# First feed-forward: three bf16 parts of its inputs in place of float32, and rows turned back one step further on

## The reference

```python
def act_quant(x):
    scale = 127.0 / jnp.clip(jnp.max(jnp.abs(x), axis=-1, keepdims=True), 1e-05)
    return jnp.clip(jnp.round(x * scale), -128, 127) / scale
def weight_quant(w):
    scale = 1.0 / jnp.clip(jnp.mean(jnp.abs(w)), 1e-05)
    return jnp.clip(jnp.round(w * scale), -1, 1) / scale
h = bit_linear(x, w1)                       # 256 -> 1024, both sides quantised
h = silu(depthwise_conv1d(h, conv_w, conv_b))   # 3 taps along the 1024 positions
return bit_linear(h, w2)                    # 1024 -> 256
```

## Time and profile before

| | us |
|---|---|
| median of 3 runs | 1917.15 (1917.0 to 1918.5) |
| profiled execution | 1919.29 |
| its span, first to last instruction | 1917.6 |
| the stage, L456 first to last update | about 185.9 to 454 |
| PE busy in the span | 1650.0 (86%) |
| DVE, ACT, POOL busy | 1160.5 (61%), 882.6 (46%), 321.8 (17%) |

### The profile page before, as it was taken

How to read it: one execution, slowest core, us unless ns; L and a number is a source line. 1 busy time by engine, 2 the same in 40 slices (tenths; PEclk the granted TensorE clock), 3 DMA queues, 4 the chain that set the end, 5 groups by cost and what they waited for, 6 DMA issues and landing times. The chain is left out here.

```text
span 1917.6 us, 29587 instructions
## 1 busy us (share of the span) xinstructions
PE 1650.0 (86%) x10149; PEld 1250.2 (65%) x10149; DVE 1160.5 (61%) x2579; ACT 882.6 (46%) x1795; POOL 321.8 (17%) x359
## 2 busy tenths in 40 slices
PE   7797789887899898799997489999936999979998
PEld 5454345556676665688885289999935888854446
DVE  4668567676456566889886823222257898842116
ACT  2332577764532221466653355555544666533213
POOL 0000000000000001211100345555562111001110
PEclk9898899998899999999998689999977999979999
DMA  6000000003000000100004812222261000010002
GB/s 200 1 1 1 1 1 1 1 1 126 1 1 1 1 1 1 31 2 1 2 1 162 322 59 72 73 73 70 72 198 28 1 2 1 2 47 0 0 1 89
DMA packets 62849, 78.83 MB, mean 41 GB/s; under 512 B 13179, under 2 KB 52655, under 8 KB 62319
## 3 DMA queue, kind: packets, MB, share of 16 engines
q1 hardware_dynamic: 42967, 47.35, 7.4%
q0 software_dynamic: 7584, 20.72, 3.4%
q10 hardware_dynamic: 12152, 8.85, 1.5%
HBM read 58.16 MB, written 18.74 MB: 40 GB/s over the span
## 5 line engine op out<-in xcount | busy, mean ns | idle before, releaser
L3003 PEld LDWEIGHTS moe_bank<-moe_xt,moe_w1e 128*128 128x128 f32 x1264 | 155.0, 194 | 5.8 <-DVE moe_xt L2851 1.8
L3003 PE MATMUL moe_bank<-moe_xt,moe_w1e 128*128 128x128 f32 x1264 | 155.8, 277 | 1.1 <-DVE moe_xt L2851 1.1
L3013 PE MATMUL moe_bank<-moe_w,moe_xin 128*128 x632 | 149.3, 379 | 0.0
L3077 ACT ACTIVATE moe_xin<-moe_bank,moe_b 128x128 f32<-128x128 f32 x316 | 90.3, 368 | 125.0 <-PE moe_bank L3003 124.9
L372 PE MATMUL l0f_hb<-l0f_xt,f_w 128*128 128x512 f32 x256 | 125.8, 623 | 5.3 <-DVE l0f_a L306 3.8
L1472 POOL TENSOR_TENSOR all_x<-all_x,l1x_fbias 128x256 f32<-128x256 f32 x32 | 23.4, 735 | 597.6 <-DVE l1x_fxn L204 597.6
L3013 PEld LDWEIGHTS moe_bank<-moe_w,moe_xin 128*128 128x128 f32 x632 | 114.0, 190 | 12.3
L209 DVE BATCH_NORM_STATS2 all_stats<-all_x 128x6 f32<-128x256 f32 x256 | 104.0, 421 | 5.2
L2860 DVE TENSOR_TENSOR moe_y<-moe_bank,moe_b2r 128x256 f32<-128x256 f32 x79 | 33.5, 425 | 118.7 <-PE moe_bank L3013 118.7
L2920 POOL DMA_INDIRECT moe_results<-moe_y,moe_row x79 | 78.0, 988 | 125.1 <-DVE moe_y L2860 121.8
L2851 DVE COPY moe_xt<-moe_bank 128x256 f32<-128x256 f32 x79 | 33.6, 425 | 106.6 <-PE moe_bank L2991 106.6
(11 more groups left out here) (484 smaller groups left out, 3812.7 us busy)
## 6 DMA issues: line engine op xcount, KB each, us to landing
moe_w<-in_L_ffn_W SPq DMA_DIRECT2D x32, 512.0 KB, 10.5
moe_w<-moe_results SPq DMA_DIRECT2D x16, 512.0 KB, 8.7
all_x<-in_x SPq DMA_DIRECT2D x4, 1024.0 KB, 12.6
out_x<-all_x SPq DMA_DIRECT2D x8, 512.0 KB, 2.9
f_w<-in_L_ffn_w_T SPq DMA_DIRECT2D x2, 1024.0 KB, 13.1
moe_inputs<-moe_xin ACTq DMA_DIRECT2D x8, 256.0 KB, 7.2
moe_inputs<-moe_w1e ACTq DMA_DIRECT2D x8, 256.0 KB, 7.8
moe_b2r<-in_L_ffn_b SPq DMA_DIRECT2D x1, 2048.0 KB, 14.1
```

What stands on the lines that cost most here:

```text
L3003: ins = nc.tensor.matmul(out, w1e[:, at:at + P], xt[:, u, c * P:(c + 1) * P], start=(c == 0), stop=(c == DC - 1))
L3013: ins = nc.tensor.matmul(bank[4 + u][:, 0:D], ht[:, u, c * P:(c + 1) * P], w2[:, ds(e * (HC * D) + c * D, D)], start=(c == 0), stop=(c == ...
L3077: ins = nc.scalar.activation(ht[:, u, m * P:(m + 1) * P], bank[1 + u][:, m * P:(m + 1) * P], ACT.Gelu, bias=b1[:, ds(e * HC + m, 1)])
```

## The change

The turned inputs are kept as float32 `xt` for one batch and as three bf16 planes `xs`: the value rounded to bf16, the rest rounded to bf16, and the rest of that. Each half of `up` is now DC x 3 = 6 bf16 matmuls against w1 in bf16 (`w1b`). For the first batch ScalarE and VectorE make the planes; for the others GpSimd does, with four instructions in a chain for each pair of tiles; `up` waits for `xs_ready`. `turn_back`, `copy_q` and `down` work on tile t-2 in place of t-1, `update` and `stats` on t-3, and there is one step more. `zq` has two buffers. ScalarE does copy_q of half 0 ahead of quantise_x and centre.

```diff
-                for t in range(TB):
+                def rest(t):
+                    dve.wait_ge(s.xt_ready, t + 2)
+                    nc.vector.tensor_tensor(rows(t), rows(t), plane(t, 0), ALU.subtract).then_inc(s.rest_ready, 2)
+                def low(t):
+                    dve.wait_ge(s.mid_ready, t + 2)
+                    nc.vector.tensor_tensor(plane(t, 2), rows(t), plane(t, 1), ALU.subtract).then_inc(s.xs_ready, 2)
...
+                for t in range(0, TB + 2, 2):
+                    if t < TB:
+                        rest(t)
+                    if t >= 2:
+                        low(t - 2)
                 norm_range(nc, c, sh, TB, T)
...
+            @block.gpsimd
+            def _(pool):
+                k = Chain(pool, s.split_step)
+                for t in range(TB, T, 2):
+                    pool.wait_ge(s.xt_ready, t + 2)
+                    if t % TB == 0 and t >= 2 * TB:
+                        pool.wait_ge(s.h_ps, (t // TB - 1) * M)
+                    k.link(nc.gpsimd.tensor_copy(plane(t, 0), rows(t)))
+                    k.link(nc.gpsimd.tensor_tensor(rows(t), rows(t), plane(t, 0), ALU.subtract))
+                    k.link(nc.gpsimd.tensor_copy(plane(t, 1), rows(t)))
+                    nc.gpsimd.tensor_tensor(plane(t, 2), rows(t), plane(t, 1), ALU.subtract).then_inc(s.xs_ready, 2)
...
                     if half == 0:
-                        pe.wait_ge(s.xt_ready, (b + 1) * TB)
+                        pe.wait_ge(s.xs_ready, (b + 1) * TB)
...
                     for d in range(DC):
-                        ins = nc.tensor.matmul(hb[g % 2][:, half * 512:(half + 1) * 512], w1[:, d, m * P:(m + 1) * P],
-                                               xt[:, b % 2, d, half * 512:(half + 1) * 512], start=(d == 0), stop=(d == DC - 1))
+                        for k in range(3):
+                            ins = nc.tensor.matmul(hb[g % 2][:, half * 512:(half + 1) * 512], w1[:, d, m * P:(m + 1) * P],
+                                                   xs[:, b % 2, k, d, half * 512:(half + 1) * 512],
+                                                   start=(d == 0 and k == 0), stop=(d == DC - 1 and k == 2))
...
-                    if 0 <= t - 1 < T:
-                        turn_back(t - 1, 0, fed)
+                    if 0 <= t - 2 < T:
+                        turn_back(t - 2, 0, fed)
...
-                        turn_x(fed, max(0, 2 * t))
+                        turn_x(fed, max(0, 2 * (t - 1)))
...
                 def copy_x(t):
                     act.wait_ge(s.xt_ps, t + 2)
+                    if t < TB:
+                        nc.scalar.activation(pair(plane(t, 0)), turned(t), ACT.Copy)
+                    else:
+                        act.wait_ge(s.xs_ready, t - TB + 2)
+                    nc.scalar.activation(pair(rows(t)), turned(t), ACT.Copy).then_inc(s.xt_ready, 2)
+                def middle(t):
+                    act.wait_ge(s.rest_ready, t + 2)
+                    nc.scalar.activation(plane(t, 1), rows(t), ACT.Copy).then_inc(s.mid_ready, 2)
...
-                for g in range(END + 2):
+                for g in range(END + 3):
                     t = g - LAG
                     b, m = g // M, g % M
+                    if 0 <= t - 2 < T:
+                        copy_q(t - 2, 0)
                     if b < B - 1 and m >= HM:
                         quantise_x((b + 1) * TB + 2 * (m - HM))
                         quantise_x((b + 1) * TB + 2 * (m - HM) + 1)
                     if 1 <= g <= SLOTS:
                         centre(g - 1)
-                    if 0 <= t - 1 < T:
-                        copy_q(t - 1, 0)
-                        copy_q(t - 1, 1)
+                    if 0 <= t - 2 < T:
+                        copy_q(t - 2, 1)
...
-                    nc.vector.tensor_scalar(f.w1[:, :, :], f.w1[:, :, :], -1.0, None, ALU.max)
+                    nc.vector.tensor_scalar(f.w1b[:, :, :], f.w1[:, :, :], -1.0, None, ALU.max)
```

More of the change, by code:

```diff
@@ L228, in stage_l0_ffn @@
         norm_sems(s)
-        w1, w2, w2q, wscale, wmean = f.w1, f.w2, f.w2q, f.wscale, f.wmean
+        w1, w2, w2q, wscale, wmean = f.w1b, f.w2, f.w2q, f.wscale, f.wmean
         xn, am, sc, inv1 = f.xn, f.am, f.sc, f.inv1
@@ L232, in stage_l0_ffn @@
         am2, sc2, inv2 = (s.sb(n, [P, T]) for n in ("am2", "sc2", "inv2"))
-        xt = s.sb("xt", [P, 2, DC, S])
+        xt = s.sb("xt", [P, DC, S])
+        xs = s.sb("xs", [P, 2, 3, DC, S], BF16)
         a = s.sb("a", [P, 3, S])
         z = s.sb("z", [P, RING, S])
-        zq = s.sb("zq", [P, 2, HM * P])
+        zq = s.sb("zq", [P, 2, 2, HM * P])
         q2 = s.sb("q2", [P, 2, M, P], BF16)
@@ L243, in stage_l0_ffn @@
         for n in ["small_loaded", "w2_scaled", "w2_ready", "table_loaded",
-                  "rstd_ready", "norm_ready", "step", "insc_ready", "q1_ready", "xd_ready", "xt_ps", "xt_ready", "h_ps", "a_ready",
+                  "rstd_ready", "norm_ready", "step", "insc_ready", "q1_ready", "xd_ready", "xt_ps", "xt_ready", "rest_ready", "mid_ready", "split_step", "xs_ready", "h_ps", "a_ready",
                   "conv_ready", "z_ready", "am2_step", "sc2_ready", "inv2_ready", "zt_ps", "zq_ready", "back_ps", "q2_ready", "y_ps",
@@ L248, in stage_l0_ffn, with rows, plane @@
         tg = sh.gates[:, 4:5]
+        def rows(t):
+            j = t % TB
+            return xt[:, :, j * P:(j + 2) * P]
+        def plane(t, k):
+            b, j = t // TB, t % TB
+            return xs[:, b % 2, k, :, j * P:(j + 2) * P]
         def z_bank(t):
@@ L326, in stats @@
                     tile_stats(nc, sh, t).then_inc(s.stats_ready, 1)
-                for g in range(END + 3):
+                for g in range(END + 4):
                     t = g - LAG
                     b, m = g // M, g % M
-                    if 0 <= t - 2 < T:
-                        update(t - 2)
+                    if 0 <= t - 3 < T:
+                        update(t - 3)
                     if 1 <= g <= SLOTS:
@@ L344, in _ @@
                             input_scales(b + 1)
-                    if 0 <= t - 2 < T:
-                        stats(t - 2)
+                    if 0 <= t - 3 < T:
+                        stats(t - 3)
                     if g == 2:
@@ L401, in turn_back @@
                     for i in range(HM):
-                        ins = nc.tensor.transpose(back_bank(t, half)[:, i * P:(i + 1) * P], zq[:, half, i * P:(i + 1) * P], sh.ident[:, :])
+                        ins = nc.tensor.transpose(back_bank(t, half)[:, i * P:(i + 1) * P], zq[:, t % 2, half, i * P:(i + 1) * P], sh.ident[:, :])
                     ins.then_inc(s.back_ps, 1)
@@ L425, in _ @@
                         turn_z(t, 1)
-                    if 0 <= t - 1 < T:
-                        turn_back(t - 1, 0, fed)
+                    if 0 <= t - 2 < T:
+                        turn_back(t - 2, 0, fed)
                     if g < SLOTS:
                         up(g, 0)
-                    if 0 <= t - 1 < T:
-                        turn_back(t - 1, 1, fed)
+                    if 0 <= t - 2 < T:
+                        turn_back(t - 2, 1, fed)
                     if 0 <= t <= TAIL:
@@ L437, in _ @@
                     if b < B - 1 and m >= HM:
-                        turn_x(fed, max(0, 2 * t))
+                        turn_x(fed, max(0, 2 * (t - 1)))
                         fed += 2
-                    if 0 <= t - 1 < T:
-                        down(t - 1)
+                    if 0 <= t - 2 < T:
+                        down(t - 2)
             @block.scalar
@@ L456, in quantise_x, with turned, pair @@
                     nc.scalar.activation(xn[:, j, :], xn[:, j, :], ACT.Copy, bias=MAGIC, scale=sc[:, j:j + 1]).then_inc(s.q1_ready, 1)
+                def turned(t):
+                    return back[:, :].rearrange("p (t c n) -> p t c n", t=2, n=P)
+                def pair(ap):
+                    return ap.rearrange("p c (t n) -> p t c n", n=P)
                 def copy_x(t):
-                    b, j = t // TB, t % TB
                     act.wait_ge(s.xt_ps, t + 2)
[L461 to L464, removed]
+                    if t < TB:
[6 more added lines that the diff above has]
+                    nc.scalar.activation(plane(t, 1), rows(t), ACT.Copy).then_inc(s.mid_ready, 2)
                 def centre(g):
@@ L480, in quantise @@
                     act.wait_ge(s.sc2_ready, t + 1)
-                    if t:
-                        act.wait_ge(s.back_ps, 2 * (t - 1) + half + 1)
-                    nc.scalar.activation(zq[:, half, :], z_bank(t)[:, half * HM * P:(half + 1) * HM * P], ACT.Copy, bias=MAGIC,
+                    if t >= 2:
+                        act.wait_ge(s.back_ps, 2 * (t - 2) + half + 1)
+                    nc.scalar.activation(zq[:, t % 2, half, :], z_bank(t)[:, half * HM * P:(half + 1) * HM * P], ACT.Copy, bias=MAGIC,
                                          scale=sc2[:, t:t + 1]).then_inc(s.zq_ready, 1)
@@ L494, in _ @@
                     quantise_x(t)
```

(8 more changed lines are left out.)

## The result

The changed kernel takes 1953.09 us (median of 4 runs, 1949.47 to 1958.29) against 1917.43: ratio 1.0185, 95% interval 1.0169 to 1.0201. The forecast was 1946, and slower. The profiled execution took 1953.58 with a span of 1951.8, 34.2 more than before. The stage itself, from ScalarE's first operation to VectorE's last update, went from 267.6 us (185.94 to 453.50) to 304.2 (182.03 to 486.19), +36.6. The stage ahead, which holds only the rounding of w1 into another buffer as a change, ended 3.9 us sooner; the stages behind took 1.5 us more. The stage begins between 178 and 186 us in the profiled runs of this study, so I compare stages by their own length.

The account below looks back on a forecast made before the run. A ring on ScalarE and VectorE, not TensorE, was taken to bound the stage; 10.6 + 3.5 + 8.4 + 3.6 + 2.7 = +28.8 us on the profiled 1919.3 gave 1948.1, forecast 1946 as run median, range 1931 to 1961.

Parts of the forecast that it names:

- The product is worth 0: TensorE's cheaper bf16 product relieves it of 27 us in 32 slots but shortens no step.
- my 0.85 a slot: TensorE's predicted relief from the bf16 product: 0.43 us a half, 0.85 a slot.
- Copy_q, +10.6: ScalarE's copy_q half 0, between quantise and centre, costs 0.48 us in each of 22 steps: +10.6.
- So it starts at once: Copy_q half 0 would not wait for turn_back, whose input is a step old, and costs only its 0.48 us.
- My clock rival: TensorE, idling more, falls to half clock, lengthening input steps, turn_x and batch starts: +12 us, 1958; chance 14%.
- Batch starts, 3.5 + 8.4: Product waits for GpSimd's split: +3.5 us at batch 2, 4.2 each at batches 3 and 4, +8.4.
- Start, +3.6: First slot: second copies, rest, middle and low, with norm_range queued behind, delay centre(0) by 3.6 us.
- Tail, +2.7: Stage's end: ring through TensorE keeps its step length; one added step without turn_z costs 2.7 us.
- The port: VectorE's dequantise could be locked out by GpSimd's last product; at a split of 4.6 us it costs 0.
- The rival's mechanism: GpSimd is slow, 6.0 us or more a split, and meets VectorE's dequantise: 1958; chance 15%.
- Range and sign: Whole kernel: 1931 to 1961 us; slower 93%, faster by over 0.2% 4%, within it 3%.
- the ring: Quantise, centre, conv, largest value, quantise again on ScalarE and VectorE: 6.55 us a plain step, 8.35 with inputs.

Follow-up runs that it names:

- e2: Changed kernel with turn_back, copy_q and down back on tile t-1 and both copy_q behind centre, three bf16 parts kept; stage 18.5 us longer than before.
- e3: Changed kernel with copy_q half 0 put back behind centre; plain and input steps those of the kernel before, to 0.01 us.
- e1: Kernel before with only the later rows and ScalarE's new order, product and inputs in float32; stage 22.2 us longer than before.
- e5: Changed kernel with norm_range ahead of VectorE's rest and low operations; centre(0) came at 20.09 us, later by 1.8; ran once, total not compared.
- e6: Changed kernel without GpSimd's fourth operation for batches 2 to 4, product taking the second part twice; batch starts 2.9 us shorter in all, stage 1.0 shorter.
- v1: Changed kernel with centre ahead of quantise and both copy_q behind quantise_x, ahead of norm and silu; plain steps 5.78 us.
- v2: Kernel before with later rows, float32 product and no split, plus centre ahead of quantise and both copy_q ahead of norm and silu; ratio 0.9926 to before.

## Why the prediction was right, and where it was not

1. *The product is worth 0.* Right: e2, with the cheap product, has the plain and input steps of before to 0.01 us. TensorE's busy time fell without one shorter step, from 146.3 us before to 137.1 in e2, between the conv of slot 8 and that of slot 31. That is less than the 20 us that my 0.85 a slot makes for these slots; the mean granted clock there was 1.00 before and 0.95 in e2.
2. *Copy_q, +10.6.* Right in size: 0.48 in each plain step, and e3 takes it out. In two steps VectorE's input scales hid 0.3 of it.
3. *"So it starts at once."* The failed step, and the larger part of the 7 us by which the forecast was short. I looked at the age of turn_back's input and not at its output: turn_x and turn_back share one bank, so copy_q of half 0 waits for turn_back, which waits for copy_x. It costs 0.92 in each input step, and 1.38 where TensorE is at half clock: the six whole input steps gave +10.3 where I had 2.9. My clock rival had the place and about the price (8 us in the steps with inputs) but the wrong cause for three quarters of these 7.4 us: 0.92 in each of the six is there in e1 too, with float32 products, and only 0.46 in four of them goes with the clock.
4. *Batch starts, 3.5 + 8.4.* Measured 3.06 and, over both steps of a change, 5.33 and 5.31, less 0.96 each for copy_q twice: 3.06 + 8.7. The sum is near, and partly by luck. Of each 5.3, e1 has 1.7 without any split: two copy_q, and 0.7 that is the wait of point 3 again. So the split's own part in the changed kernel is 3.6, where I had 4.2. Within it two errors nearly cancel: GpSimd's chain is 3.8 us with hand-overs (382.12 to 385.93), at my lower bound and not 4.6, and TensorE's part behind it ran nearly at half clock (4.8 us from product to largest value, where full clock makes 2.8 and I had 3.9).
5. *Start, +3.6.* Measured 3.53. The order was as forecast: norm_range ends 17.2 us after the stage's start (17.4 in the forecast), the norms follow, and centre(0) comes behind them without a wait for TensorE. What norm_range alone costs isn't settled (e5).
6. *Tail, +2.7.* Measured 3.9. The extra step is 2.74 as forecast. The other 1.2 lie in its first steps: the quantise of tiles 23 to 26 start at distances of 5.52, 3.58 and 3.83 us where they were 5.32, 2.51 and 3.84. Tiles up to 23 use the one bank for turning back, and with t-2 one more of them does so after the last product; that this is the cause is read from the order, not tested. It isn't a fixed price either: e1, e3 and e6 have their rows on tile t-2 as well and tails of 42.7 to 42.8, 1.0 to 1.1 longer still, and why stays open.
7. *The port.* The rule of the Trainium skill, "SBUF — State Buffer", "Who interferes with whom", had no case to bite in the changed kernel: in the input step above GpSimd's chain ends at 294.3 and dequantise starts at 296.2, and all 24 dequantise take 343 to 351 ns. GpSimd's two-tensor operations took 1152 to 1158 ns, 1.77 us never. But v1 moves dequantise beside the chain, and there the pair takes 1.36 us in six steps and 0.93 in three, not 0.61 as in v2, which has the same order and no GpSimd. So far v1 agrees with the rule; that the port is the cause isn't isolated, nor whether it lengthened v1's steps. The rival's mechanism was there, then, and the order of the changed kernel kept clear of it. From v1:

```profile
285.53 1.16 POOL L383 TENSOR_TENSOR l0f_xt<-l0f_xt,l0f_xs 128x512 f32<-128x512 f32 x1
...
286.15 1.36 DVE L300 TENSOR_SCALAR f_xn<-f_xn,f_inv 128x256 f32<-128x256 f32 x2
...
286.75 0.61 POOL L384 CAST l0f_xs<-l0f_xt 128x512 bf16<-128x512 f32 x1
```

8. *Range and sign.* 1953 lies in 1931 to 1961. In the profiled executions the stage grew by 36.6 us, 7.8 more than the sum: 7.4 are point 3 in the whole input steps, 1.5 its share at the starts of batches 3 and 4, 1.2 point 6, against smaller terms that came out low (1.2 for the split at these two starts, 0.4 at batch 2, 0.6 hidden copy_q).

## What to carry to other kernels

Find the ring first: follow one step from an operation to the same operation a step later, and sum; an engine that is 88% busy but not in it, as TensorE here, gives nothing back. Before moving an operation ahead in an in-order queue, ask not only whether its input is old enough but who else uses the buffer that its producer writes. Here the cheaper product shortened steps only in an order that put TensorE into the ring, and even there the work that prepares it, standing ahead of a point where everything waits (the first slot of each batch), cost more than it gave.

## What the runs showed of the hardware

GpSimd's subtraction of two tensors of 512 columns took 1154 ns on average (1152 to 1158), with bf16 in or out alike, below the 1263 ns that was its least in the earlier trace rows; a rounding copy to bf16 took 610 ns, as the float32 copy there. TensorE's granted clock went from 1.00 on average to 0.89 between slots 9 and 31, and a group of four transposes took 1.09 or 0.63 us by it; behind the wait at the start of batch 2 the window from 245 to 250 us shows 0.50, the lower level of 1.2 GHz, as the Trainium skill has it in "TensorE: Matmul & The Clock Gate", "The HAM clock gate". So a stall ahead of TensorE was paid twice here, once as the wait and once in the slower work behind it (4.8 us where full clock makes 2.8, in batch 4). VectorE's dequantise, 343 to 351 ns an operation otherwise, took up to 751 ns beside GpSimd's operations in v1.
